# GpSimd makes the base of each partial sum, the square comes ahead of the energy, eleven VectorE taps in four halves

## The reference, cut to what matters

```python
dyn_w = dyn.reshape(b * c, 1, 5, 5)                 # a 5x5 kernel of its own per image and channel
out = conv_general_dilated(x, dyn_w, ...)           # depthwise
u = out.mean(1); s2 = square(out - u).mean(1)
out = (out - u) * rsqrt(s2 + EPS)                   # norm over the 64 channels
out = gelu(einsum('bchw,oc->bohw', out, w_expand))  # 64 -> 256 channels
gx = sqrt(sum(square(out), axis=(2, 3)))            # energy of a channel over the whole image
out = g * (out * gx / (gx.mean(1) + EPS)) + bt + out
out = einsum('bohw,co->bchw', out, w_shrink) + x    # 256 -> 64
```

## Time and profile before

| | us |
|---|---|
| runs | 837.55, 838.02, 840.32 |
| median | 838.02 |
| the profiled execution, its own time | 838.94 |
| its span | 837.0 |
| layer 0 | 0 to 502 |
| statistics of half 5 (slot 6) to statistics of half 13 (slot 14), 8 slots | 143.98, or 18.00 each |
| the same of half 4 (slot 5) to half 5 (slot 6) | 18.34 |
| PE, DVE, ACT, POOL busy over the span | 779.9, 620.8, 407.4, 467.8 |

### The profile page before, as it was taken

The page is one execution under the profiler, slowest core; times in us unless marked ns, Lnnn a source line. Parts: engine busy times, 40 slices in busy tenths (PEclk is TensorE's granted clock), DMA queues, the critical chain, the costliest instruction groups (busy, mean ns, idle before and its releaser), DMA issues. The chain is left out here.

```text
span 837.0 us, 15644 instructions
## 1 busy us (share of the span) xinstructions
PE 779.9 (93%) x5399; PEld 637.4 (76%) x5399; DVE 620.8 (74%) x1137; ACT 407.4 (49%) x497; POOL 467.8 (56%) x458
## 2 busy tenths in 40 slices
PE   5999999999999999999999988787899999999886
PEld 5999998999998999999999986544444444444332
DVE  4666666666665666667888878998799898989875
ACT  5591003777772000000000006379999999999871
POOL 2333333333333333336888884888889889898610
PEclk9999999999999999999999996989999999999999
DMA  6760000000000000000000002132233443433224
GB/s 145 158 176 0 0 0 1 1 0 0 0 0 2 0 0 0 0 0 2 0 0 0 0 0 50 44 83 57 53 79 82 93 106 85 103 78 82 60 69 102
DMA packets 61572, 35.81 MB, mean 43 GB/s; under 512 B 41504, under 2 KB 59488, under 8 KB 61536
## 3 DMA queue, kind: packets, MB, share of 16 engines
q1 hardware_dynamic: 61536, 35.36, 17.9%
HBM read 17.85 MB, written 9.37 MB: 33 GB/s over the span
## 5 line engine op out<-in xcount | busy, mean ns | idle before, releaser
L481 PE MATMUL psum<-line_hi,taps_hi 128*128 128x256 f32 x1270 | 202.9, 292 | 11.7 <-DVE taps_lo L377 8.4
L495 PE MATMUL psum<-line_lo,taps_hi 128*128 128x256 f32 x1270 | 202.5, 291 | 0.8 <-DVE line_lo L430 0.8
L489 PE MATMUL psum<-line_hi,taps_lo 128*128 128x256 f32 x1270 | 202.0, 291 | 0.0
L430 DVE SCALAR_TENSOR_TENSOR line_lo<-psum,rest 128x256 fp32r<-128x256 f32 x254 | 108.2, 426 | 123.7 <-POOL rest L262 115.4
L481 PEld LDWEIGHTS psum<-line_hi,taps_hi 128*128 128x128 f32 x1270 | 177.1, 192 | 12.8 <-issue 9.2
L495 PEld LDWEIGHTS psum<-line_lo,taps_hi 128*128 128x128 f32 x1270 | 176.4, 191 | 2.0 <-DVE line_lo L430 1.8
L262 POOL TENSOR_TENSOR rest<-x,line_hi 128x256 f32<-128x256 f32 x127 | 82.8, 652 | 168.3 <-DVE line_hi L421 168.3
L489 PEld LDWEIGHTS psum<-line_hi,taps_lo 128*128 128x128 f32 x1270 | 176.7, 191 | 0.0
L771 POOL TENSOR_TENSOR part<-part,prod 128x960 f32<-128x960 f32 (+2 forms) x64 | 145.2, 2269 | 18.5 <-ACT prod L838 11.3
L262 POOL TENSOR_TENSOR rest<-by_h,line_hi 128x256 f32<-128x256 f32 x127 | 91.5, 720 | 83.4 <-DVE line_hi L421 83.4
L314 ACT ACTIVATE by_h<-x (+1 forms) x128 | 85.7, 670 | 105.9 <-DVE x L410 104.2
(11 more groups left out here) (159 smaller groups left out, 761.6 us busy)
## 6 DMA issues: line engine op xcount, KB each, us to landing
stage<-in_x_dram SPq DMA_DIRECT2D x32, 256.0 KB, 4.1
rstd_wide<-rstd_dram SPq DMA_DIRECT2D x30, 256.0 KB, 5.4
out_dram<-x SPq DMA_DIRECT2D x28, 256.0 KB, 5.5
crossed<-x SPq DMA_DIRECT2D x16, 256.0 KB, 3.5
crossed<-x SPq DMA_DIRECT2D x16, 240.0 KB, 3.3
out_dram<-x SPq DMA_DIRECT2D x8, 128.0 KB, 2.5
rstd_dram<-rstd SPq DMA_DIRECT2D x15, 64.0 KB, 1.5
fc_in<-in_L_conv_w_fc_dram SPq DMA_DIRECT2D x2, 100.0 KB
```

The costliest lines, as they stand in the source:

```text
L430: dve.scalar_tensor_tensor(out=line_lo[:, (slot + 1) % SLOTS, :, part], in0=as_lines(line_ps[slot][:, 0:LINE]), scalar=0.0, in1=as_lines(r ...
L481: mm = pe.matmul(line_ps[slot][:, 0:LINE], taps_hi[:, s, d, :], line_hi[:, slot, :, d:d + WP], start=(d == 0), stop=(d == OFFSETS - 1))
L489: pe.matmul(line_ps[slot][:, 0:LINE], taps_lo[:, s, d, :], line_hi[:, slot, :, d:d + WP], start=False, stop=False, skip_group_check=True)
L495: mm = pe.matmul(line_ps[slot][:, 0:LINE], taps_hi[:, s, d, :], line_lo[:, slot, :, d:d + WP], start=False, stop=(d == OFFSETS - 1), skip_ ...
```

## The change

GpSimd makes the base (a multiplication of an image by a number per partition, `base`), after `norm`, and ScalarE's products begin at 1. Halves 2 to 5 have an eleventh VectorE tap (the tap `("up", 3)`, in the last place but one) and one product and one addition less. On ScalarE `square` comes ahead of `add_squares` at the head of a slot. On TensorE `conv(3)` comes ahead of the second expand and no longer behind it. The stores of the last two halves are issued by SP and ScalarE, one parity each, and no longer all by SP.

```diff
+EARLY, EARLY_TAP = (2, 3, 4, 5,), ("up", 3)
+def dve_taps(u):
+    return DVE_TAPS[:-1] + [EARLY_TAP] + DVE_TAPS[-1:] if u in EARLY else DVE_TAPS
+def act_taps(u):
+    return [t for t in ACT_TAPS[u % 2] if u not in EARLY or t != EARLY_TAP]
...
 sync: for u in range(LAST - 1, UNITS):
     for c in range(2):
-        store_chunk(u, c)                 # both parities
+        store_chunk(sp, u, c, 0)
...
 gpsimd:
+            def base(u):
+                src, rows, cols, weight = place(u, *act_taps(u)[0])
+                if u > 1:
+                    pool.wait_ge(tap_step, taps_end(u - 2))
+                pool.tensor_scalar(part[:, u % 2, rows, cols], src, weight, None, ALU.mult).then_inc(base_ready, 1)
...
+                base(s)
-                for n in range(1, N_ACT):
+                for n in range(1, len(act_taps(s))):
                     add_product(s, n)
...
 scalar:
+                if w in range(UNITS):
+                    square(w)
                 if n in range(UNITS):
                     add_squares(n, 1)
-                if w in range(UNITS):
-                    square(w)
-                if s + 1 < UNITS:
-                    product(s + 1, 0)
...
             root_energy(B - 1)
+            for u in range(LAST - 1, UNITS):
+                for c in range(2):
+                    store_chunk(act, u, c, 1)
...
 tensor:
                 conv(2)
+                conv(3)
                 at_e(0, 1)
-                conv(3)
```

More of the change, by code:

```diff
@@ L62, with taps_end, prods_end, parts_end @@
 ACT_TAPS = [MIDDLE + SIDES, MIDDLE[::-1] + SIDES]
+EARLY, EARLY_TAP = (2, 3, 4, 5,), ("up", 3)
[3 more added lines that the diff above has]
+    return [t for t in ACT_TAPS[u % 2] if u not in EARLY or t != EARLY_TAP]
+def taps_end(u):
+    return sum(len(dve_taps(i)) + 1 for i in range(u + 1))
+def prods_end(u):
+    return sum(len(act_taps(i)) for i in range(u + 1))
+def parts_end(u):
+    return sum(len(act_taps(i)) - 1 for i in range(u + 1))
 def build(nc, x, k_td, k_dt, k_lr, k_rl, fc1, ln1_w, ln1_b, fc2, ln2_w, ln2_b,
@@ L555, in sem @@
             return ctx.enter_context(nc.semaphore(name))
-        N_DVE, N_ACT = len(DVE_TAPS) + 1, len(ACT_TAPS[0])
-        PART_STEPS = N_ACT - 1
+        PART_STEPS = len(ACT_TAPS[0]) - 1
         VAR_STEPS = 2
@@ L625, in block_two @@
         part_step = sem("part_step")
+        base_ready = sem("base_ready")
         squared = sem("squared")
@@ L692, in resp_col, with store_chunk @@
             return stat_ps[:, 2 * STAT_COLS:2 * STAT_COLS + 1] if b < B - 1 else psum[:, 3, 0:1]
+        o = out.rearrange("b c (j p) w -> b p c j w", p=2)
+        def store_chunk(queue, u, c, p):
+            b, j = u // 2, ROWS * (u % 2) + CROWS * c
+            queue.wait_ge(finished, 2 * u + c + 1)
+            queue.dma_start(o[b, p][:, j:j + CROWS, :], x[C * p:C * p + C, b, j:j + CROWS, :]).then_inc(stored, 16)
         block = ctx.enter_context(nc.Block())
@@ L697, in _ @@
         def _(sp):
-            o = out.rearrange("b c (j p) w -> b p c j w", p=2)
             def cross(u):
@@ L702, in cross @@
                 if u >= 2:
-                    sp.wait_ge(tap_step, N_DVE * (u - 1))
+                    sp.wait_ge(tap_step, taps_end(u - 2))
                 lo, hi = max(ROWS * h - 1, 0), min(ROWS * (h + 1) + 1, HP)
@@ L714, in store @@
                     sp.dma_start(o[b, p][:, j:j + ROWS, :], x[C * p:C * p + C, b, j:j + ROWS, :]).then_inc(stored, 16)
[L716 to L720, removed]
             def spread_rstd(u):
@@ L771, in add_part @@
                 pool.tensor_tensor(dst, dst, other, ALU.add).then_inc(part_step, 1)
-            def add_product(u, n):
[L774 to L777, removed]
+            def base(u):
[3 more added lines that the diff above has]
+                pool.tensor_scalar(part[:, u % 2, rows, cols], src, weight, None, ALU.mult).then_inc(base_ready, 1)
+            def add_product(u, n):
+                _, rows, cols, _ = place(u, *act_taps(u)[n])
+                pool.wait_ge(prod_ready, parts_end(u - 1) + n)
+                if n == 1:
+                    pool.wait_ge(base_ready, u + 1)
+                else:
+                    pool.wait_ge(part_step, parts_end(u - 1) + n - 1)
                 add_part(u, rows, cols, prod[:, n - 1, rows, cols])
@@ L800, in make_spread @@
             def make_spread():
-                pool.wait_ge(tap_step, N_DVE * LAST)
+                pool.wait_ge(tap_step, taps_end(LAST - 1))
                 for k in range(SUBS):
@@ L828, in product @@
             def product(u, n):
[L829 to L837, removed]
+                src, rows, cols, weight = place(u, *act_taps(u)[n])
+                if u >= 1:
+                    act.wait_ge(part_step, parts_end(u - 2) + min(n, len(act_taps(u - 1)) - 1))
+                dst = prod[:, n - 1, rows, cols]
                 act.activation(dst, src, ACT.Copy, scale=weight).then_inc(prod_ready, 1)
             def square(u):
-                act.wait_ge(tap_step, N_DVE * (u + 1))
+                act.wait_ge(tap_step, taps_end(u))
                 if u > 0:
@@ L913, in _ @@
                     for p in between:
-                        if s + 1 < UNITS:
+                        if s + 1 < UNITS and p < len(act_taps(s + 1)):
                             product(s + 1, p)
@@ L952, in add_part @@
             def add_part(u):
-                dve.wait_ge(part_step, PART_STEPS * (u + 1))
-                dve.wait_ge(tap_step, N_DVE * u + N_DVE - 1)
+                dve.wait_ge(part_step, parts_end(u))
+                dve.wait_ge(tap_step, taps_end(u) - 1)
                 if u >= INNERS:
@@ L960, in take_tap @@
             def take_tap(u, i):
-                if i == N_DVE - 1:
+                if i == len(dve_taps(u)):
                     return add_part(u) if u > 0 else add_first_part()
-                src, rows, cols, weight = place(u, *DVE_TAPS[i])
+                src, rows, cols, weight = place(u, *dve_taps(u)[i])
                 if i == 0:
@@ L967, in take_tap @@
                 else:
-                    dve.wait_ge(tap_step, N_DVE * u + i)
+                    dve.wait_ge(tap_step, taps_end(u - 1) + i)
                 if u == 0:
@@ L981, in second_chunk @@
                                        weight, None, ALU.mult))
-                for i in range(N_DVE - 2):
+                for i in range(len(DVE_TAPS) - 1):
                     src, rows, cols, weight = place(0, *DVE_TAPS[i])
@@ L989, in add_first_part @@
             def add_first_part():
-                dve.wait_ge(part_step, PART_STEPS)
+                dve.wait_ge(part_step, parts_end(0))
                 dve.wait_ge(conv_done, 2)
-                dve.wait_ge(tap_step, N_DVE - 1)
+                dve.wait_ge(tap_step, taps_end(0) - 1)
                 second = inner[:, 0, CROWS:ROWS, :]
@@ L1118, in take @@
                     if s in range(UNITS):
-                        for i in range(taken[0], min(taken[0] + n, N_DVE)):
+                        for i in range(taken[0], min(taken[0] + n, len(dve_taps(s)) + 1)):
                             take_tap(s, i)
@@ L1139, in _ @@
                     respond(n // 2)
-                take(N_DVE)
+                take(len(DVE_TAPS) + 2)
             finish(LAST - 4, 0)
@@ L1198, in convolve @@
                     if u >= 2:
-                        pe.wait_ge(tap_step, N_DVE * (u - 1))
+                        pe.wait_ge(tap_step, taps_end(u - 2))
                         pe.wait_ge(xlo_ready, u - 1)
@@ L1238, in widen @@
                     pe.wait_ge(spread_made, SUBS)
-                    pe.wait_ge(tap_step, N_DVE * UNITS)
+                    pe.wait_ge(tap_step, taps_end(LAST))
                 for g in range(2):
@@ L1253, in expand @@
                 if e == FREE_CONV + 1:
-                    pe.wait_ge(tap_step, N_DVE * LAST)
+                    pe.wait_ge(tap_step, taps_end(LAST - 1))
                 if 0 < e <= FREE_CONV:
```

## The result

The changed kernel takes 849.11 us (median of four runs, 848.32 to 849.87), the kernel before 837.78 beside it. The ratio is 1.0126, with a 95% interval of 1.0111 to 1.014: **11 us slower**, where 3.5 us faster was forecast, and outside the range of 831.7 to 839.0. The profiled execution has a span of 847.5 us and took 849.19.

What follows compares the result with a forecast made beforehand. With every engine nearly full, loops of waits were taken to bound the kernel, in steady slots TensorE's exchange with ScalarE after the change. Terms -2.9 - 0.2 + 0.5 - 0.5 - 0.4 = -3.5 gave 834.5 us, range 831.7 to 839.0.

Steps and rivals of the forecast that it cites:

- The base: GpSimd's new multiplication of 1024 numbers: put at 1.2 us, between a cast's 1.04 and a two-input product's 2.38, costing nothing.
- if the base is over 1.9: Stated sign of being wrong: GpSimd's base instruction taking more than 1.9 us.
- The room: GpSimd, steady pairs of slots: a base costs nothing up to (36.1 - 32.3)/2 = 1.9 us each.
- a dear base: Rival, GpSimd: base at 2.38 us makes its pair 37.1, 0.5 a slot over eight slots, 838.5 us; chance 0.12.
- the early slots: Slots 2 to 4: gains of 1.5, 2.1 and 0.9, 4.5 together, less 1.6 for one clock fall: -2.9 us.
- TensorE's new order, steady slots: Slots 6 to 14: exchange with ScalarE's gelus sets 18.05 to 18.1 us a slot against 18.00, +0.5 over eight.
- the loop through VectorE: Expand, five matmuls, `respond`, then taps up to the variance 12.1 us later; seen as the second loop of waits.
- the blocks: Early slots summed from traced TensorE and ScalarE block lengths at full clock: 15.5, 16.4 and 18.3 us.
- Two or three falls: Rival: TensorE's clock falls two or three times in slots 2 to 4, 836.5 to 838.0 us; chance 0.25.
- one fall: TensorE's clock, slot 3: one fall expected, as its second pause is nearest to those that fell; costs 1.6 us.
- The end: Slot 14 onward: earlier `respond` gives -0.5 us, last stores shared by two issuing queues -0.4.
- The slow rival: Rival: TensorE's clock falls in steady slots at the new 1.2 us pause, 2.0 each, 842.5 at four; chance 0.07.

Runs made afterwards that it cites:

- e1: Kernel before with only the base moved to GpSimd, the other four parts of the change undone: 851.29 us, ratio 1.0161 to the kernel before.
- e5: Changed kernel with GpSimd multiplying the base by the constant 0.5 instead of the partition's tap, output differing: 850.74 us in one run.
- e4: Changed kernel with the base on GpSimd written as a product of two tensors, the tap broadcast: 837.46 us, ratio 0.999 to the kernel before.
- e2: Changed kernel with GpSimd copying the base without its tap's factor, so output is not right: 834.8 us, ratio 0.996 to the kernel before.
- e3: Changed kernel with the base back on ScalarE, other four parts kept: 837.05 us, ratio 0.9995 to the kernel before.
- e6: e2 with conv(3) again behind the second expand: 833.51 us, ratio 0.9942 to the kernel before.
- e7: Changed kernel with GpSimd making only odd halves' bases, as two-tensor products, conv(3) behind second expand, one product between first gelus: 834.62 us, ratio 0.9956.
- e12: Kernel before with VectorE taking one tap more before it waits for respond, nothing else: 837.32 us, ratio 0.998.
- e8: e2 without the eleventh VectorE taps, ten in every half: 835.74 us, ratio 0.9957 to the kernel before.
- e9: e7 with VectorE taking one tap more before it waits for respond: 829.62 us, ratio 0.9891 to the kernel before.

## Why the prediction was wrong, point by point

**The base: the step that failed.** "I take 1.2, since the base has one large input as the cast has." The nearest rows gave 1.04 and 2.38, and the truth, 2.85, lies beyond both ends (e1, e5). The two rows differ in the operation, not only in the number of inputs, and I had no row of that operation at all. The range of the price should have been open at the top: with two unlike neighbours nothing says that the unknown lies between them. The prediction's own sign of being wrong, "if the base is over 1.9", was met.

The room was right, (36.1 - 32.3)/2 = 1.9 (e4 with 1.89: 0.1 us a slot). So the rival "a dear base" had the right mechanism, the right place and the right threshold. Only its price was too low, 2.38, and with it its time, 838.5; it had 0.12 of the chance. At 2.85, and with the gap of 0.15 behind the base that the prediction left out, its own sum gives 38.3 a pair, 1.1 a slot above the 36.1, and 834.5 + 8.8 = 843.3.

Most of the other 5.8 us are in slots 1 to 6, which lost 1.9 us where 3.1 was to be gained. Of these 5.0, 3.1 go with the price of the base: the same slots take 88.30 in e2, 88.35 in e4 and 91.36 in the changed kernel, in one profile each. Whether GpSimd's lateness or the clock behind it makes them wasn't separated. The other 1.9 are missing in e2 too, and are the subject of the early slots below.

The Trainium skill ("GPSIMD Engine Reference", section 4.1) calls one-input operations roughly line rate. The trace agrees for the copy and the cast (1.04 us) and contradicts it for the multiplication by a number (2.77 to 2.85). The advice of the same section of the Trainium skill to leave elementwise arithmetic to VectorE holds here: a VectorE tap, which multiplies and adds, takes 1.2 us.

**TensorE's new order, steady slots: right, 18.05 to 18.1 against 17.99 measured** (e2), 0.5 us too much in eight slots, which is what it was given as a loss. The mechanism was as forecast: in e2's slot 9 the third expand starts 7.83 after T (7.87 forecast) behind a pause of 1.22 (1.2 forecast), the first expand of that slot being at 679.52:

```profile
687.35 1.13 PE L1289 MATMUL psum<-normed,expand_w 64*128 64x512 f32 x4 [1.22 <-ACT wide L894]
```

That removing ScalarE's base brings nothing there is shown by e2 and e3 (143.95, 143.94, 143.98). What I had incomplete is why 36.0 stays: I named the loop through VectorE and then didn't count it. e6, e7 and e12 show three loops, TensorE's exchange with ScalarE among them, within 0.2 us a slot of each other.

**The early slots: the blocks in part right, the clock wrong.** In e2, where the price is out of the way, slots 2, 3 and 4 take 15.54, 19.04 and 19.58. The blocks were put at 15.5, 16.4 and 18.3. The difference is the clock: it fell in both slots, and the first time its lower level lasted longer than in the kernel before. Windows of e2:

```profile
574.00:584.00 10.00, 8.17 (x22) 4.03 (x20) 7.96 (x7) 6.82 (x7) 4.94 (x3) 0.66 0.33 79
594.00:601.00 7.00, 5.66 (x20) 3.74 (x18) 6.07 (x10) 5.82 (x6) 6.62 (x5) 0.76 0.28 75
```

and the third expand of slot 3, with the pause ahead that the prediction had put at 1.9:

```profile
576.74 2.08 PE L1289 MATMUL psum<-normed,expand_w 64*128 64x512 f32 x4 [1.83 <-ACT wide L894]
```

The gain of slots 1 to 6 was 1.2 us there and not 3.1. "Two or three falls" was the right rival, for this execution of e2.

The reason that the prediction gave for one fall doesn't hold. It read off that pauses of 2.11 and 2.20 bring the clock down and 1.49 does not, and then went by the length of each pause. In e6 a pause of 2.33 in slot 3 was not followed by a fall (the expand behind it and the next took 1.13 each, and the clock was 1.00 from 570 to 587), in e12 one of 2.12 was not, and a pause of 1.88 in slot 2 was followed by one in e8 and not in e2. Slots 2 to 4 have one fall in e6 and e12, two in the kernel before, e2 and the changed kernel, three in e3 and e8. e6's slots 2 and 3, at full clock and in TensorE's old order, take 15.53 and 16.34, close to the 15.5 and 16.4 of the prediction's blocks. What decides a fall besides the pause is open, and so is how many are typical of one program, since each has one profile.

**The end: right in direction, its size within the scatter.** 0.9 was forecast for `respond` and the stores; e2 has 1.1 and the changed kernel 2.1. From slot 14's statistics to those of half 15 e2 takes 31.67 and before 32.09, the 0.4 of the earlier `respond`; e6, with the old order of TensorE, has 32.09 again. What comes after the statistics of half 15 takes 37.37 before and from 35.2 to 37.3 in the profiles of the kernels with shared stores, so the stores' part can't be told from the scatter.

**The slow rival** (the clock falls in steady slots) didn't happen where it was priced: e2 has 136.4 us of busy TensorE in 144 and a slot of 17.99 throughout. In the changed kernel it did, behind GpSimd's lateness.

**In all:** the price of the base was one number, used sixteen times, and it made the forecast wrong. With a cheap base the other terms come to -1.2, 0 and -1.1 in e2's profile, -2.3 where -3.5 was forecast, and its median is 4.1 below that of the kernel before beside it. That this median, 834.8, is so near to 834.5 is in part luck: the traced parts fall short by 1.2, and the median of ten executions goes beyond by 0.6.

## What to carry to other kernels

An operation that no row of the trace shows has no price between its neighbours. Where sixteen or more of them go onto an engine whose pair of slots has only 3.7 us of pauses, work out the price from which it decides (here 1.9) and treat the chance of exceeding it as the main question, or measure one instruction first. And when several loops are within 1% of each other, shortening one shows almost nothing: the reward comes when all of them are shortened at once and every engine keeps some room, as in e9.

## What the runs showed of the hardware

- GpSimd's multiplication of 128x1024 f32 numbers by one number took 2.85 us with the number per partition and 2.77 with a constant. The same product with a broadcast second tensor took 1.89, and a copy 1.04. Of the three products the one with the single tensor to read was the slowest.
- GpSimd's `norm`, also a product of two tensors of this size, took 2.38. With a broadcast operand the product is shorter by a fifth.
- TensorE's clock: in e2 a pause of 1.15, an expand of 1.13 and a pause of 1.83 were followed by 0.66 of the clock on average over 10 us. The length of a pause doesn't settle it: 1.88 was followed by a fall in e8 and not in e2, 2.11 was in the kernel before and 2.12 was not in e12, which is the same program up to there, and 2.33 was not in e6.
